# Cross attention written out as one row of 32 rounds, and the banded head's weights in four transfers

## The reference, cut to what matters

```
# stage 4, banded attention: 16 heads of 32 over 4 key heads, window of 64 keys backward
q, k, v = x @ Wq.T + bq, x @ Wk.T + bk, x @ Wv.T + bv
q, k = rope(rmsnorm(q, qn_w)), rope(rmsnorm(k, kn_w))
x = layernorm(x + softmax(mask(q k^T * scale)) v @ Wo.T + bo)

# stage 5, cross attention: 16 heads of 128, four sequences of 512 tokens and 512 context rows of 256
q = rmsnorm((x @ Wq).reshape(B, S, 16, 128), gq)      # Wq 512 x 2048
k = rmsnorm((ctx @ Wk).reshape(B, S, 16, 128), gk)    # Wk, Wv 256 x 2048
v = (ctx @ Wv).reshape(B, S, 16, 128)
x = layernorm(x + (softmax(q k^T / sqrt(128)) v) @ Wo)  # Wo 2048 x 512
```

## Time and profile before

| | |
|---|---|
| median of 3 runs | 2571.3 us (2570.89 to 2572.88) |
| the profiled execution's own time | 2571.21 us |
| its span, first to last instruction | 2569.4 us |
| mean granted TensorE clock | 0.945 |
| busy: PE, PEld | 2187.9 us (85%), 1555.7 us (61%) |
| busy: DVE, ACT, POOL | 1408.9, 1207.9, 909.8 us |
| banded attention | from 777.6 us to 1166.1 us of the span |
| cross attention | from 1166.1 us to 2300.6 us of the span |

### The profile page before, as it was taken

How to read it: one execution, slowest core, us unless ns; L and a number is a source line. 1 busy time by engine, 2 the same in 40 slices (tenths; PEclk the granted TensorE clock), 3 DMA queues, 4 the chain that set the end, 5 groups by cost and what they waited for, 6 DMA issues and landing times. The chain is left out here.

```text
span 2569.4 us, 36165 instructions
## 1 busy us (share of the span) xinstructions
PE 2187.9 (85%) x12664; PEld 1555.7 (61%) x12664; DVE 1408.9 (55%) x2138; ACT 1207.9 (47%) x2272; POOL 909.8 (35%) x569
## 2 busy tenths in 40 slices
PE   5989989867895787795999999999999999967772
PEld 4555646446774665554777767777777677744340
DVE  4656666644545435542555665557556755552637
ACT  3636464534324635534555545554555555531513
POOL 3525242410003202203455455555555555530101
PEclk9999999988897999997999999999999999988886
DMA  2000000010001000003111211121111111111001
GB/s 109 1 1 1 1 1 1 1 62 1 1 1 48 1 1 1 1 1 117 36 38 49 74 49 49 49 73 33 41 49 49 49 49 49 49 37 69 1 1 65
DMA packets 62367, 84.15 MB, mean 33 GB/s; under 512 B 6132, under 2 KB 41332, under 8 KB 61752
## 3 DMA queue, kind: packets, MB, share of 16 engines
q1 hardware_dynamic: 62264, 82.76, 9.5%
HBM read 74.36 MB, written 4.19 MB: 31 GB/s over the span
## 5 line engine op out<-in xcount | busy, mean ns | idle before, releaser
L1925 DVE RECIPROCAL s_inv_sums<-banks 128x512 f32<-128x512 f32 x64 | 214.8, 3356 | 343.3 <-PE banks L2038 340.0
L1799 POOL TENSOR_TENSOR s_qk_rstd<-s_mean_sq,minus_half 128x8 f32<-128x8 f32 x64 | 118.7, 1854 | 502.0 <-DVE s_mean_sq L1912 502.0
L2031 PE MATMUL banks<-s_probsT,s_v 128*128 128x512 f32 x512 | 231.2, 594 | 0.0
L1862 ACT ACTIVATE s_probsT<-banks,s_minus_bound,s_qk_rstd 128x512 f32<-128x512 f32 x256 | 177.0, 782 | 92.5 <-PE banks L200 88.5
L594 DVE TENSOR_REDUCE s_neg_max<-banks 128x1 f32<-128x512 f32 x256 | 165.4, 684 | 87.9 <-PE banks L660 86.3
L543 ACT ACTIVATE s_probsT<-banks 128x512 f32<-128x512 f32 x256 | 148.7, 600 | 81.5 <-PE banks L674 79.1
L1833 ACT ACTIVATE s_squares<-banks 128x512 f32<-128x512 f32 x64 | 38.2, 597 | 288.0 <-PE banks L200 287.9
L198 PE MATMUL banks<-s_w_proj_hi,xT_hi 128*128 (+1 forms) x512 | 170.8, 334 | 2.9 <-DVE s_ctxT_lo L1973 2.9
L2031 PEld LDWEIGHTS banks<-s_probsT,s_v 128*128 128x128 f32 x512 | 97.6, 191 | 111.1 <-issue 108.5
L1792 POOL TENSOR_TENSOR s_w_proj_lo<-s_w_proj_raw,s_w_proj_hi 128x2048 f32 (+1 forms) x33 | 152.0, 4607 | 14.0 <-ACT s_w_proj_hi L1825 14.0
L1808 POOL TENSOR_TENSOR s_probs_pair_sums<-s_probsT 128x1024 f32<-128x1024 f32 x64 | 151.0, 2360 | 7.2 <-issue 7.2
(11 more groups left out here) (409 smaller groups left out, 5896.4 us busy)
## 6 DMA issues: line engine op xcount, KB each, us to landing
s_w_proj_raw<-l1x_wq SPq DMA_DIRECT2D x33, 512.0 KB, 4.6
s_w_out_raw<-l1x_wo SPq DMA_DIRECT2D x33, 512.0 KB, 3.6
s_w_proj_raw<-l1x_wk SPq DMA_DIRECT2D x33, 256.0 KB, 4.8
s_w_proj_raw<-l1x_wv SPq DMA_DIRECT2D x33, 256.0 KB, 5.1
x_all<-x SPq DMA_DIRECT2D x4, 1024.0 KB, 12.3
s_ctxT<-ctxT SPq DMA_DIRECT2D x8, 512.0 KB, 5.7
x_cur<-x_all SPq DMA_DIRECT2D x4, 1024.0 KB, 7.7
out<-x_all SPq DMA_DIRECT2D x4, 1024.0 KB, 4.3
```

What stands on the lines that cost most here:

```text
L1799: pool.tensor_tensor(rs[:, j, :, :], ms[:, j, :, :], c.mhalf[:, 0:T * HP].rearrange("p (t h) -> p t h", h=HP), ALU.pow) \
L1862: act.activation(probsT[:, h, k, :], pb.ap(("e", h, k)), ACT.Exp, bias=bound[:, 0:1], scale=rs[:, 1, k, h:h + 1]).then_inc(pb.freed(("e", ...
L1925: dve.reciprocal(inv[:, h, :], pb.ap(("sum", h))).then_inc(pb.freed(("sum", h)), 1)
L2031: mm = pe.matmul(pb.ap(("o", h)), v[:, k, h * DX:(h + 1) * DX], probsT[:, h, k, :], start=(k == 0), stop=(k == T - 1))
```

## The change

Three things are changed.

1. **The cross attention is one list.** `seq` names every piece of all 32 rounds (and half rounds at both ends) in one order; every engine walks it and issues its part, with no loop on the chip. Q is half of the queries, KV a quarter of the keys and values, TK and TQ the transposes, E a quarter of a head's scores, U the adding up of probabilities, V the values, SU the sums, R the reciprocal, M its product, OH the split of the outputs, O an output piece; WQ, WK, WO are the weights' high parts, WKl and WOl the low ones; MQ and MK the mean squares, NQ the queries' norm. Output pieces of round `j - 1` now stand between pieces of rounds `j` and `j + 1`, and NQ stands between R and M of head 0.
2. **Borders and norm.** The tokens are transposed directly from `x_all` (X) two rounds before their sequence starts, with no transfer. Statistics of the layer norm follow each output piece, and ACT normalises (LX). The output weights' low part comes later in POOL's order. The projections use two banks (0 and 1), scores, outputs and half of X three (2 to 4), values 5 and 6, sums 7. `x_cur` holds squares and probability sums.
3. **The banded head.** Its weights come in four transfers, each with its own copy, and the subtractions are dealt to DVE (0, 2, 3) and POOL (1). PE no longer waits for the clearing of `kT` before the first transposes.

```diff
-            sp.dma_start(w[:, :, :], d["l1a_wqkvT"].rearrange("(k p) n -> p k n", p=P)).then_inc(weights, 16)
+            for k in range(KD):
+                sp.dma_start(w[:, k, :], d["l1a_wqkvT"].rearrange("(k p) n -> p k n", p=P)[:, k, :]).then_inc(weights[k], 16)
...
-            pool.memset(kT[STK:P, :, :].bitcast(F32), 0.0).then_inc(zeros_set, 1)
+            pool.wait_ge(w_hi, 2)
+            pool.tensor_tensor(w_l[:, 1, :], w[:, 1, :], w_h[:, 1, :].bitcast(F32), ALU.subtract).then_inc(w_lo_pool, 1)
             pool.drain()
-            pool.wait_ge(w_hi, 1)
-            pool.tensor_tensor(w_l[:, 0:2, :], w[:, 0:2, :], w_h[:, 0:2, :].bitcast(F32), ALU.subtract).then_inc(w_lo_pool, 1)
+            pool.memset(kT[STK:P, :, :].bitcast(F32), 0.0).then_inc(kT_cleared, 1)
+            pool.drain()
 
...
-            act.activation(w_h[:, :, :], w[:, :, :], ACT.Copy).then_inc(w_hi, 1)
+            for k in range(KD):
+                act.wait_ge(weights[k], 16)
+                act.activation(w_h[:, k, :], w[:, k, :], ACT.Copy).then_inc(w_hi, 1)
...
-            dve.wait_ge(w_hi, 1)
-            dve.tensor_tensor(w_l[:, 2:KD, :], w[:, 2:KD, :], w_h[:, 2:KD, :].bitcast(F32), ALU.subtract).then_inc(w_lo_dve, 1)
+            for k in (0, 2, 3):
+                dve.wait_ge(w_hi, k + 1)
+                dve.tensor_tensor(w_l[:, k, :], w[:, k, :], w_h[:, k, :].bitcast(F32), ALU.subtract).then_inc(w_lo_dve, 1)
...
-            pe.wait_ge(zeros_set, 1)
...
+                    if b == 0 and t == 0 and lo == 0:
+                        pe.wait_ge(*((w_lo_pool, 1) if k == 1 else (w_lo_dve, {0: 1, 2: 2, 3: 3}[k])))
...
+        seq = [("X", 0, k) for k in range(KD)] + [("WQ", 0), ("Cx", 0), ("WK", 0), ("WKl", 0)]
+        for j in range(-1, N + 1):
+            now, nxt, prv, border = 0 <= j < N, j + 1 < N, 0 <= j - 1, (j + 2) % G == 0 and j + 2 < N
+            if now:
+                seq += [("E", j, 0, k) for k in range(T)] + [("U", j, 0)]
+            if nxt:
+                seq.append(("Q", j + 1, 0))
+            if now:
+                for k in range(T):
+                    seq.append(("E", j, 1, k))
+                    if prv and k < HP:
+                        seq.append(("OH", j - 1, k))
+                seq += [("U", j, 1), ("V", j, 0)]
+            elif prv:
+                seq += [("OH", j - 1, h) for h in range(HP)]
+            if j + 2 < N:
+                seq.append(("WQ", j + 2))
+            if nxt:
+                if (j + 1) % G == 0 and j > 0:
+                    seq.append(("Cx", (j + 1) // G))
+                seq += [("Q", j + 1, 1), ("MQ", j + 1)]
+            if now:
+                seq += [("SU", j, 0), ("R", j, 0)]
+            if j + 2 < N:
+                seq.append(("WK", j + 2))
+            if now:
+                seq.append(("WO", j))
+            if border:
+                seq += [("X", (j + 2) // G, k) for k in range(KD)]
+            if j % G == 1 and j > G:
+                seq.append(("LX", j // G - 1))
+            if nxt:
+                seq.append(("NQ", j + 1))
+            if now:
+                seq.append(("M", j, 0))
+            if prv:
+                seq.append(("O", j - 1, 0))
+            if now:
+                seq.append(("V", j, 1))
+            if nxt:
+                seq.append(("KV", j + 1, 0))
+            if now:
+                seq.append(("SU", j, 1))
+            if nxt:
+                seq += [("KV", j + 1, 1), ("TQ", j + 1, 0), ("KV", j + 1, 2)]
+            if j + 2 < N:
+                seq.append(("WKl", j + 2))
+            if now:
+                seq.append(("WOl", j))
+            if prv:
+                seq.append(("O", j - 1, 1))
+            if nxt:
+                seq += [("TQ", j + 1, 1), ("KV", j + 1, 3), ("MK", j + 1)]
+            if prv:
+                seq.append(("O", j - 1, 2))
+            if nxt:
+                seq.append(("TK", j + 1, 0))
+            if prv:
+                seq.append(("O", j - 1, 3))
+            if nxt:
+                seq.append(("TK", j + 1, 1))
+            if now:
+                seq += [("R", j, 1), ("M", j, 1)]
+            if prv and j % G == 0:
+                seq.append(("L", j // G - 1))
+        seq.append(("LX", B - 1))
+
+        uses, na, nb = [], 0, 0
+        for s in seq:
+            if s[0] in ("Q", "KV", "TK", "TQ") or s[0] == "X" and s[2] % 2:
+                uses.append((s, na % 2, 1))
+                na += 1
+            elif s[0] in ("E", "O", "X"):
+                uses.append((s, 2 + nb % 3, 1))
+                nb += 1
+            elif s[0] == "V":
+                uses.append((s, 5 + s[2], 1))
+            elif s[0] == "SU":
+                uses.append((s, 7, 1))
+        ps.open(uses)
...
+            load_q(0)
+            load_ctx(0)
+            load_kv(0)
             sp.dma_start(gains[:, 0, :], d["l1x_gq"].broadcast_to([P, DX])).then_inc(consts, 16)
             sp.dma_start(gains[:, 1, :], d["l1x_gk"].broadcast_to([P, DX])).then_inc(consts, 16)
             sp.dma_start(gcols[:, 0:1], d["l1x_gq_col"]).then_inc(consts, 16)
             sp.dma_start(gcols[:, 1:2], d["l1x_gk_col"]).then_inc(consts, 16)
-            load_proj(sp, 0)
-            load_out(sp, 0)
...
+                elif ph == "U":
+                    h = s[0]
+                    pool.wait_ge(*ps.released(0, ("E", j, h, T - 1)))
+                    if j > 0:
+                        pool.wait_ge(*ps.full(0, ("SU", j - 1, h)))
+                    pool.tensor_tensor(psum[:, h, :], probs[:, h, 0, :], probs[:, h, 1, :], ALU.add)
+                    pool.drain()
+                    pool.tensor_tensor(psum[:, h, :], psum[:, h, :], probs[:, h, 2, :], ALU.add)
+                    pool.drain()
+                    pool.tensor_tensor(psum[:, h, :], psum[:, h, :], probs[:, h, 3, :], ALU.add).then_inc(p_sum.sem, 1)
+                    pool.drain()
...
+                elif ph == "R":
+                    h = s[0]
+                    dve.wait_ge(*ps.full(0, ("SU", j, h)))
+                    if j > 0:
+                        dve.wait_ge(*o_lo.after(j - 1, h + 1))
+                    dve.reciprocal(inv[:, h, :], ps.ap(("SU", j, h))).then_inc(ps.freed(("SU", j, h)), 1)
+                elif ph == "M":
+                    h = s[0]
+                    dve.wait_ge(*ps.released(0, ("SU", j, h)))
+                    dve.wait_ge(*ps.full(0, ("V", j, h)))
+                    dve.tensor_tensor(inv[:, h, :], ps.ap(("V", j, h)), inv[:, h, :], ALU.mult) \
+                       .then_inc(ps.freed(("V", j, h)), 1)
...
+                    if j % G == G - 1:
+                        dve.drain()
+                        dve.bn_stats(c.stats[:, t, :], xt)
+                        if t == T - 1:
+                            dve.drain()
+                            for u in range(T):
+                                dve.bn_aggr(c.mv[:, u, :], c.stats[:, u, :])
+                            dve.drain()
+                            dve.tensor_scalar(c.veps[:, :], c.mv[:, :, 1], 1e-5, None, ALU.add).then_inc(var_ready.sem, 1)
```

More of the change, by code:

```diff
@@ L1786, in _ @@
+            sp.wait_ge(consts, 64)
         @block.gpsimd
         def _(pool):
[L1788 to L1795 removed]
@@ L1864, in body @@
[L1864 to L1873 removed]
+                        sqr.then_inc(squared["k"].sem, 1)
+                    act.activation(kk[:, t, :], kv[:, 0:NW], ACT.Copy)
@@ L1889, in start @@
-            def start(b):
-                c.act_x_hi(act, b, (b, b * G), pa)
-                act.wait_ge(*ctx_in.after(b, 16))
-                act.activation(c_h[:, :, :], cT[:, :, :], ACT.Copy).then_inc(ctx_hi.sem, 1)
-            turns(act, start, body, nothing)
+                        xt = c.x[:, j * T + t, :]
+                        act.activation(xt, xt, ACT.Identity, bias=nmr[:, t:t + 1], scale=c.rstd[:, t:t + 1])
         @block.vector
         def _(dve):
-            dve.wait_ge(consts, 64)
@@ L2027, in values @@
-                def values(h):
-                    pb.wait_empty(pe, y, ("o", h))
-                    for k in range(T):
-                        pe.wait_ge(*pb.released(y, ("e", h, k)))
-                        mm = pe.matmul(pb.ap(("o", h)), v[:, k, h * DX:(h + 1) * DX], probsT[:, h, k, :],
-                                       start=(k == 0), stop=(k == T - 1))
-                    mm.then_inc(pb.filled(("o", h)), 1)
-                def sums(h):
-                    pb.wait_empty(pe, y, ("sum", h))
-                    pe.wait_ge(*p_sum.after(y, h + 1))
-                    pe.matmul(pb.ap(("sum", h)), c.ones[:, :], psum1[:, h, :], start=True, stop=True) \
-                      .then_inc(pb.filled(("sum", h)), 1)
@@ L2052, in body @@
-                if x is not None:
-                    queries(0)
-                if y is not None:
-                    sums(0)
-                    values(1)
-                    sums(1)
-                if x is not None:
-                    queries(1)
-                    for t in range(T):
```

(7 more changed lines are left out.)

579 lines of the change are left out of this document (285 added, 294 removed).

## The result

The changed kernel takes 2548.64 us (median of 4 runs, 2546.97 to 2550.66) against 2571.2 us (median of 4 runs), a ratio of 0.9911 (95% interval 0.9899 to 0.9923): 22.6 us faster. The forecast was 2537.7 with a range of 2520 to 2560, so the time lies in the range, just inside the own range of the likeliest case, with 22.6 of the 33.5 us that the sum promised. The profiled execution took 2548.6 us, its span is 2546.8 us. Against the profiled execution of before (2571.21) the program's pieces compare as follows; a piece ends where the next begins, and the distances are between rows of the two traces.

A forecast was written before the change was run, and what follows sets the result against it. PE was taken to bound the rounds, busy 48.9 of 50 us. Terms 1.4 - 11.6 - 9.7 - 6.0 + 0.4 - 8.0 = -33.5 against 2571.21 gave 2537.7 us; range 2520 to 2560, likeliest case's own 2527 to 2549.

The forecast's parts named there:

- the steady rounds: Cross attention's steady rounds: the old wait goes, a new one comes at the third piece of keys; +1.4 us over 30 rounds.
- New round: 32.6 + 0.81: Steady round: PE's own content of 32.6 us plus 0.81 of wait and refill gives 33.4, 0.05 more than before.
- the start: Start of the cross attention: queries start earlier, first scores at 1194.0 instead of 1203.72; -9.7 us, bounds -12 to -6.
- the 18 named as a sign: Sign of being right: first scores about 18 us earlier in the span, 8 from the band and 10 from the start.
- PE waits about 2.7 us for it: Cross attention's start: PE waits about 2.7 us for the queries' norm, now ahead of the third piece of keys.
- The first round: First round of the cross attention: no output pieces, earlier keys' root; 30.3 us instead of 36.3, -6.0 us, bounds -3 and -6.5.
- The band: Start of the banded attention: earlier transposes, transfers and bias row; bias matmul at about 790.7, -8.0 us, bounds -5 and -9.
- Borders: Three borders between sequences: 2.9 us each, together 8.8 against 20.4; -11.6 us, bounds -15.2 and -5.4.
- A second wait: Rival: a second wait per round, at the round's end or the second head's fourth bank; +15 us, 2553 us, 22 in 100.
- The wait at the keys: Rival, no wait at the keys: ACT frees the bank within 0.5 us, rounds of 32.7; -21 us, 2517 us, 9 in 100.
- The borders did what they say: Rival: PE stops at borders and ends as long as before, for banks, weights or context; 2557 us, 8 in 100.
- The instruction stream: Rival: without a loop PE waits for instruction packets behind weight loads once a round; +71 us, 2609 us, 6 in 100.

The follow-up runs named there:

- the run with another bank: The changed kernel with the transposes of the queries' first head in banks 2 to 4 instead of 0 and 1; 2520.20 us, ratio 0.9801.
- The run without one square: The changed kernel with the squares of keys' piece 1 left out of the keys' mean squares; 2537.46 us, ratio 0.9865.
- the first experiment: The kernel before with only the banded attention's part of the change, its cross attention still in a loop; 2565.88 us, ratio 0.9975.
- late low part: The changed kernel with POOL's low part of the second round's key weights moved behind round 0's keys' mean squares; 2546.20 us, ratio 0.9900.

## Why the prediction was right, and where it was not

**Right in mechanism and place: the steady rounds.** The old wait was gone and one new one stood at the third piece of keys. Its loss was put at 0.81 us and measured 0.83 (33.56 less the 32.73 of the run with another bank). That the two agree so well is in part luck, for two small errors offset each other. The 1.19 us of standing still were exact: the third piece of keys starts 1.42 us behind the start of the second's last matmul (1382.65 to 1384.07), to the hundredth as in the earlier trace rows. But the four transposes cover 0.35 us of it, not 0.44 (1343.32 to 1343.67 with another bank), and the 0.06 us of refilling are not there on top.

The term came out at +6.3 us, not +1.4, because the step "New round: 32.6 + 0.81" took the old order's content for the new one. The 32.6 was right for the old order; the new order's content is 32.73. Over 30 rounds that is 3.9 us, and the 0.02 us more of hole and the rounding of a hundredth or two in the terms make up the other 1.0. PE's starts show where the 0.13 lies. From a steady round of before (from 1306.76, without its hole and refill) to one of the run with another bank (from 1319.19), scores went from 5.45 to 5.66 us, projections and output pieces from 17.71 to 18.68, values and sums from 7.78 to 6.97, transposes from 1.66 to 1.42. The spread order changes kind more often, and a first product behind transposes or sums takes 0.32 or 0.63 us to the next start instead of 0.23; most of that is won back in the group ahead of it, and how much each change of kind costs net is not shown.

**Mis-sized: the start, -6.1 instead of -9.7.** The -9.7 does not follow from its own terms, which give -11.8 + 2.7 = -9.1. The first scores came 12.3 us earlier in the span, not the 18 named as a sign. The queries started 12.5 us earlier in their stage (6.6 instead of 19.1), better than the 11.8. The step "PE waits about 2.7 us for it" failed, because it took the norm's 1.23 us from a place where POOL was idle: the wait was 4.5 us, and "They take as long as before" was 1.9 us short, 1.5 of it the clock behind the wait. In the change POOL starts the next low part at the same moment. Without that instruction there, PE's wait was 2.40 us and the start -9.6 (-12.5 + 2.4 + 0.5), near the -9.7 partly by luck. The rule was in the prediction, for the band only: the Trainium skill ("SBUF — State Buffer", section "SBUF: two separate sides") says that whichever of the two engines starts first holds the shared pair for its whole instruction. The trace agrees again: POOL from 1178.65 to 1180.99, and the norm's end at 1182.07, 1.08 us later. I had not asked what POOL does at that time in the new list.

**Missed: a hole in the first round and the clock behind it.** The first round gained 4.9 instead of 6.0 us, since its price held no hole at the keys: with another bank it took 30.57 us, near the 30.3 of the prediction. The second round began at a lower clock. In the 8 us ahead of its scores PE stood still four times (0.59, 0.59, 1.02, 0.97 us), and the clock was 0.77 in the 7.3 us from 1222.89; in the run with another bank it stood still three times (0.59, 1.02, 0.97) and the clock stayed at 1.00. The run without one square, with four waits again (the first of 0.31 us), had 0.77 too. Bounds for such a clock behind the first round were in none of my terms.

**Right within a us or two, the band in part by luck.** The band gave -7.5 for -8.0, and the first experiment places it there alone. But the bias matmul came 9.3 us earlier in its stage, not 8.0, and 1.8 us were given back behind it, 0.9 of them by the next bias matmul, at the lower clock; and with all low parts on DVE the band was worth -10.4 (378.1 against 388.5), outside the bounds of -5 to -9. So the estimate by the lock rule of the Trainium skill, which spoke against dealing the quarters out, had the right sign: dealing cost 2.9 us instead of 1, the clock included. Borders -13.4 for -11.6: 2.3 us each instead of 2.9. The end 0.0 for +0.4. The norm's place 0: behind the product it cost nothing either, and only ahead of the reciprocal 193.7 us. POOL's third addition per head and the later low weights: no hole in PE is ended by the probabilities' sums or the output weights in a steady round.

**The rivals.** A second wait did not come, but the run with the mean squares behind output addition 2 shows it one addition away. The wait at the keys was there; it went with another bank, and with output piece 0 put between, which opened another. The borders did what they say. The instruction stream moved 102 packets in place of 67 without a hole in PE from 1258 to 2238 us that only issue explains. The 0.23 us at the loop's end, which the prediction set against the Trainium skill, are no test of it: no run shows whether that branch leaves what had been fetched.

## What to carry to other kernels

When work is spread so that waits disappear, list for each bank what stands between its two uses, and compare it with the reader's whole chain; here 0.35 us of transposes against the 1.19 us that the reader needs (both from one start on PE to the next) cost 0.83 us in each steady round, and one line in the bank assignment gave back more than the whole rewrite had brought. Try another bank before another order: a piece moved into one gap uncovered what it had covered. And price an instruction from a row in which its neighbours do what they will do in the new order, POOL beside DVE above all; a wait of some 4 us on PE cost its length and then the clock behind it.

## What the runs showed of the hardware

- A DVE product of two SBUF inputs (128x1024) took 1.22 us alone, 1.97 when POOL held on 0.9 us into it in each steady round, and 3.35 to 3.38 when POOL's 2.3 us began first.
- Behind PE waits of 4.52 and 3.92 us the granted clock was 0.51 for 3.3 us and 0.80 on the mean over 15.4 us. Holes of 0.59 us once a round left it at 1.00. Behind a wait of 2.40 us it was 1.00 (late low part), behind one of 2.5 us once 1.00 and once 0.76 (first round before, and with the band alone).
- Three ACT instructions of 128x256 that empty a bank let PE go 1.03 us after the last matmul's modelled end, 1.42 us after its start; one of them fewer takes off 0.28, the start-to-start step of two, not the 0.38 that a row shows for one.
- A subtraction of 768 columns on DVE took 3.73 us for four with POOL silent (0.93 each), and 2.49 for two with POOL beside it.

```profile
782.53 3.73 DVE L1456 TENSOR_TENSOR s_wqkv_lo<-s_probsT,s_wqkv_hi 128x768 fp32r<-128x768 f32 x4
```
